# A two-layer GNN and MoE kernel: gate weights transposed one FFN step later, and smaller tiles at the end of layer 1

## What is computed

```python
x = x + gnn0(layernorm(x), edge_weight1)     # weighted mean over in-edges, [h_neigh, x] @ W.T + b
x = x + ffn0(layernorm(x))                   # 8 experts 256 -> 512 -> 256, relu, top 2, softmax
h = relu(layernorm(x) @ Wp.T + bp)           # layer 1: 128 features
agg = sqrt(segment_sum(w * h[src]**2, dst))
x = x + h @ W1.T + b1 + agg @ W2.T + b2
x = x + ffn1(layernorm(x))                   # 8 experts 256 -> 256 -> 256, gelu, residual inside
```

## Time and profile before

| | |
|---|---|
| median of three runs | 2748.9 us |
| the profiled execution | 2746.08 us, span 2744.2 us |
| mean granted TensorE clock | 0.941 |
| busy share: TensorE, VectorE, ScalarE, GpSimd | 83%, 68%, 47%, 62% |
| gather DMAs, GpSimd | 1664, mean 1.01 us |
| chain that ended last, by engine | PE 47%, POOL 24%, DVE 12%, issue 11%, ACT 4% |

### The profile page before, as it was taken

The page is one execution under the profiler, slowest core; times in us unless marked ns, Lnnn a source line. Parts: engine busy times, 40 slices in busy tenths (PEclk is TensorE's granted clock), DMA queues, the critical chain, the costliest instruction groups (busy, mean ns, idle before and its releaser), DMA issues.

```text
span 2744.2 us, 45870 instructions
## 1 busy us (share of the span) xinstructions
PE 2265.4 (83%) x16513; PEld 1420.9 (52%) x16513; DVE 1857.9 (68%) x4929; ACT 1296.2 (47%) x2221; POOL 1710.3 (62%) x1678
## 2 busy tenths in 40 slices
PE   0137999999999999999999734588878778988987
PEld 0124555555555555555558634444444444567876
DVE  8576777778778777787776644355555555667775
ACT  4023455454454554544556601244334444566667
POOL 3677666575575665764430077777777777777760
PEclk9999999999999999999999955699999999999999
DMA  5733333343333333432220032122222222222220
GB/s 208 253 104 110 102 107 103 97 120 88 98 111 92 106 103 97 118 93 82 72 64 21 32 108 62 51 63 70 69 57 63 70 70 63 63 67 71 71 61 11
DMA packets 116317, 237.92 MB, mean 87 GB/s; under 512 B 30434, under 2 KB 70364, under 8 KB 115572
## 3 DMA queue, kind: packets, MB, share of 16 engines
q0 software_dynamic: 66560, 163.68, 21.3%
q1 hardware_dynamic: 49524, 71.26, 7.7%
HBM read 209.16 MB, written 25.67 MB: 86 GB/s over the span
## 4 chain that ended last, share of the span: by engine, by line
PE 47%; POOL 24%; DVE 12%; issue 11%; ACT 4%; DMA 2%; DVEq 0%; POOLq 0%; ACTq 0%; SPq 0%
POOL ring L625 23%; PE psY L757 18%; PE psH L721 17%; PE psM L821 4%; PE psE L703 2%; DVE hsc L1334 1%; PE psE L711 1%; DVE hid L1328 1%; DMA ring<-table,src_s 1%; PE psM L773 1%; PE psE L731 1%; PE psE L705 1%; PE psM L781 1%; ACT L1506 1%; DVE wbuf L1074 1%
## 5 line engine op out<-in xcount | busy, mean ns | idle before, releaser
L625 POOL DMA_INDIRECT ring<-table,src_s x1664 | 1680.7, 1010 | 902.4 <-issue 624.1
L721 PE MATMUL psH<-xnT,wbuf 128*128 128x512 f16 (+2 forms) x4320 | 909.9, 348 | 8.3 <-ACT hid L1517 8.3
L757 PE MATMUL psY<-hsc,wbuf 128*128 128x512 f16 (+2 forms) x4320 | 902.9, 345 | 11.2 <-DVE hsc L1334 6.2
L1517 ACT ACTIVATE hid<-psH,b,scl 128x512 f32<-128x512 f32 (+2 forms) x720 | 503.4, 699 | 761.1 <-PE psH L721 757.8
L1328 DVE TENSOR_TENSOR hid<-hid,cS 128x512 f32<-128x512 f32 (+2 forms) x720 | 427.7, 594 | 452.0 <-ACT cS L1524 310.1
L757 PEld LDWEIGHTS psY<-hsc,wbuf 128*128 128x128 f16 x4320 | 415.5, 99 | 391.4 <-issue 23.6
L721 PEld LDWEIGHTS psH<-xnT,wbuf 128*128 128x128 f16 x4320 | 406.1, 102 | 300.8 <-issue 21.1
L1334 DVE TENSOR_TENSOR hsc<-hid,hsc 128x512 f16<-128x512 f32 (+2 forms) x720 | 423.1, 588 | 0.4 <-ACT hsc L1531 0.3
L711 PE MATMUL psE<-ohbuf,ring 128*128 128x40 f32 x1664 | 251.1, 306 | 186.7 <-DMA ring<-table,src_s 186.5
L1531 ACT ACTIVATE hsc<-hid 128x512 f16<-128x512 f32 (+2 forms) x720 | 392.0, 544 | 27.1 <-DVE hid L1328 26.1
L711 PEld LDWEIGHTS psE<-ohbuf,ring 128*128 128x128 f32 x1664 | 238.3, 219 | 233.4 <-DMA ring<-table,src_s 227.9
(11 more groups left out here) (163 smaller groups left out, 1938.6 us busy)
## 6 DMA issues: line engine op xcount, KB each, us to landing
ring<-table,src_s POOLq DMA_INDIRECT x1664, 2.5
wbuf<-w_in SPq DMA_DIRECT2D x2, 4096.0 KB, 20.7
wbuf<-x_in SPq DMA_DIRECT2D x7, 896.0 KB, 12.7
table<-ring SPq DMA_DIRECT2D x7, 896.0 KB, 3.6
feat<-table SPq DMA_DIRECT2D x11, 512.0 KB, 4.0
xin<-x_in SPq DMA_DIRECT2D x11, 512.0 KB, 3.9
x_d<-x SPq DMA_DIRECT2D x11, 512.0 KB, 3.5
wbuf<-w_in SPq DMA_DIRECT2D x2, 2048.0 KB, 11.2
```

The costliest lines, as they stand in the source:

```text
L625: pool.indirect_dma_start(out=l.ring[:, g % l.R, k, :], out_offset=None, in_=l.table, in_offset=bass.IndirectOffsetOnAxis(ap=src_s[:, c:c ...
L721: last = mm(psH[n % 2][:, 0:l.TT[t]], l.w1(e, i, k, c), x[:, j, k, 0:l.TT[t]], start=(k == 0 and m == 0), stop=(k == KD - 1 and m == 2))
L757: last = mm(psY[d][:, 0:l.TT[t]], l.w2(e, i, c, d), h[:, j, 0:l.TT[t]], start=False, stop=(n == l.M - 1 and m == 2))
L1517: f(hid[(l.M * t + n) % HB][:, 0:l.TT[t]], psH[n % 2][:, 0:l.TT[t]], (ACT.Relu, ACT.Gelu)[l.i], scale=l.un_up, bias=l.b1[:, n // l.HC, n % ...
```

## The change

Two edits. The transposition of the gate weights moves on TensorE from the end of step `at_comb` (29 in layer 0, 13 in layer 1) to the following step, between that step's `up` (which there is the first `up` of the next tile) and its `down`. The wait for `comb_ready` moves from the middle of that step's `down` to the head of `spread_weights` behind it. The place of `weights_copied` on ScalarE and of `gate_weights` on VectorE stays. And layer 1's list of tiles becomes eight of four, six of two, five of one: 19 tiles.

```diff
-ENDS = (([], [2, 2, 1]), ([], [2] * 8 + [1]))
+ENDS = (([], [2, 2, 1]), ([], [2] * 6 + [1] * 5))
@@ def spread_weights(l, t, e):
                 x = NX * t + e
+                if t and e == 0:
+                    pe.wait_ge(l.comb_ready, t + 1)
                 added, copied = l.spread_after[x]
@@ def down(l, t, n, at):
                     for m, (i, j) in enumerate(PARTS):
-                        if d == 0 and m == 1 and at[1] + 2 == l.M and at[0] < l.NT - 1:
-                            pe.wait_ge(l.comb_ready, at[0] + 2)
@@ the loop over steps
                             up(l, t + 1, n + 2 - l.M)
+                        if n == l.at_comb + 1 and not last:
+                            weights_transposed(l, t + 1)
                         if n:
                             down(l, t, n - 1, (t, n))
...
                             logits(l, t + 1)
-                        if n == l.at_comb:
-                            weights_transposed(l, t + 1)
```

## The result

The changed kernel takes 2758.09 us (median of 5 runs, 2754.08 to 2760.52), the kernel before in the same comparison 2745.66 us (2740.91 to 2751.58): ratio 1.0041, 95% interval 1.0023 to 1.0059, 11 us slower. The forecast was 15 us slower. Measured again later, the ratio was 1.0043 (1.0030 to 1.0055).

A forecast was written before the change was run, and what follows sets the result against it. TensorE bounds layer 0, GpSimd's gathers set layer 1's pace up to the last four-block tiles, and the tail is bound by its own instructions. 2746.08 - 13.5 - 4 + 32.4 = 2761.0 us profiled, 2764 us median; range 2746 to 2778.

The forecast's parts named there:

- Edit 1, layer 0: Layer 0's loop: the next tile's first `up` fills TensorE's wait at the transposition; 13.5 us of 16.4 gained.
- rival (c): Layer 0: the wait returns at `spread_weights` because ScalarE's copy comes late; +13.5 us, 2777.5 us; chance 0.05.
- Edit 1, layer 1: Layer 1's tail: waits ahead of the transposition get back at least an `up`; -4 us, bounds 0 and -5.
- Edit 2: Layer 1's end: blocks 44 to 48 become five tiles; tail 202.8 us, 32.4 us more than before.
- wait behind the last gather: Layer 1's end: claimed there is none for the two more tiles to shorten.
- four stretches with their ten sums: Layer 1's end: four one-block stretches of 25.5 us each, plus 6 us for 10 group sums.
- Rival (b): One-block tiles: more latency, TensorE at half clock behind stalls; 28.5 us a stretch, +12, 2776 us; chance 0.12.
- Rival (a): One-block tiles: ScalarE the only bound, sums hidden in TensorE's idle time; tail 182.4 us, median 2743.4 us; chance 0.20.
- lower bound: One-block stretch at layer 1's end: ScalarE's work alone, 21.4 us.
- The sum: Whole kernel: 2746.08 - 13.5 - 4 + 32.4 = 2761.0 us profiled; 2764 us on the median, slower by 15 us.
- second of the two rules: One-block tiles: the Trainium skill's about 81 ns per 128-column matmul gives TensorE 15.6 us; rejected for the trace's 56 ns.

The follow-up runs named there:

- layer-0-only kernel: Transposition moved in layer 0 alone, old list of tiles, against the kernel before: 2732.97 us, ratio 0.9941.
- filled kernel: Changed kernel plus matmuls adding zeros in TensorE's waits of the four one-block tiles that prepare another: 2751.56 us, against 2759.04 us of the changed kernel.
- run without the roots: Changed kernel with copies for the two square roots in preparing layer 1's tiles 15 to 18: 2742.15 us, ratio 0.9975 to the kernel before.

## Why the prediction was right, and which terms were off

**Edit 1, layer 0.** Right in mechanism and nearly in size: 13.5 us forecast, 13.8 in the first trace. The `up` covers 1.28 of 1.29 us, the wait doesn't come back at `spread_weights`, and rival (c) falls: ScalarE waits for the transposition (23.5 us in all), not TensorE for the copy. The layer-0-only kernel had 16.3 us by its median, with an interval of 3.6 us either way; by the stretches its trace has 13.7 us from the second tile on. The first tile's time varied between 112 and 116 us from trace to trace, in kernels of both kinds.

**Edit 1, layer 1.** The term was mis-sized. I took 4 us, with bounds of 0 and 5; the changed kernel's trace was 10.6 us ahead in layer 1 at 2549 us. That trace is the upper end. From layer 0's last transposition to that point the traces without the edit in layer 1 took 1039.0, 1039.5 and 1040.5 us, and the five others with it on these chips 1029.8 to 1035.3 us, so 3.7 to 9.2 us less. The five waits at L843 there, which I had priced, fell from 11.9 us before to 7.3 us in that trace, 4.6 us in all, where the `up`s in front of them are worth 3.9 (1.29 and four times 0.65 us). What I put at nothing is TensorE's own work. In the five stretches from 2355 to 2574 us before, it was busy 199.3 us, in the same ones with the moved transposition alone 191.5 us, with the same instructions: the difference is the granted clock, 0.92 to 0.97 there and 0.96 to 1.00 here. The other traces scatter, 196.1 and 199.6 us without the edit and 191.7 to 196.0 us with it. That the shorter stall keeps the clock up is argued from these columns, and no run isolates it. In the old list the gathers take most of it back; that the new list keeps it I had not seen.

**Edit 2.** The plan held: two-block stretches 37.7 and 35.0 us forecast, 0.65 less each with the moved transposition, 35.6 and 34.7 measured; the end 22.1 and 22.3. The wait behind the last gather was indeed not there: with the gathers out 26 us earlier against the end, or more, the time rose. The term that failed in size is four stretches with their ten sums: 108 us forecast, 114.3 in the first trace and 110.4 in the second. With no sums a stretch took 27.0 and 26.1 us, not 25.5, and the first two took 30.2 and 30.1 us (29.1 and 28.2) with four sums each. What I left out of the likeliest case is the half clock, 0.78 to 0.91 in these stretches. Rival (b) had it with the right place and too high a price, 12 us; the filled kernel shows 5 to 7. Rival (a), ScalarE as the only bound, falls: its work is just the 21.4 us of the lower bound, but it idles for 6 to 9 us more in each stretch. ScalarE's waits from 2620 to 2734 us, the four stretches:

```profile
ACT hsc L1531 <- DVE hid L1328: 10.0, 9, 2.1
ACT hid L1517 <- PE psH L721: 6.0, 9, 2.3
ACT yT L1543 <- PE psY L757: 5.2, 4, 1.4
ACT cT L1510 <- PE psM L843: 5.1, 4, 1.4
ACT cS L1524 <- PE psE L733: 1.4, 4, 0.8
```

They stand ahead of the FFN's own steps, of the output and of the copied gate weights; none stands ahead of a root or an exp. So ScalarE and the other two engines hand the short steps of one block to each other late; how much of that each table load causes is shown only by the run without the roots, above.

**The sum.** +32.4 - 17.5 = +14.9 forecast, +12.1 by the traces, with the gain and the loss both larger than forecast: -24.4 by 2549 us (and two smaller gains in the two stretches behind), and +36.5 after it. By medians +11 to 12 us. List alone +38 us, and the list on top of the moved transposition +31 us, where I had said 32.4. That the sum came within 3 to 4 us is in part luck: the gain was 6.9 us larger in the first trace than the 17.5 us of the forecast, and the loss 4.1 us larger than the 32.4 us, and the two offset each other. Two slips in the working are too small to matter: eleven pieces of 0.65 us that fall to 0.34 us lose 3.4 us, not 3.7, and the 15.6 us that the second of the two rules gives TensorE is below the 21.4 us of ScalarE in a tile that prepares another, not above.

What stays open: how the 31 us divide. Taking the four root loads of a tile away gives back 18 us of the changed kernel, but these loads are also there in tiles that the old list has; at 4.5 us a tile the two that were added account for half of that, 9 us. The clock comes on top (0.86 to 0.90 in the four stretches without the loads, 0.86 to 0.91 with them), so 14 to 16 us of 31 are named. The rest, 15 to 17 us, may be the remaining latency of two more preparations; no run took it apart. And what holds up all engines on the slow chip is open.

## What to carry to other kernels

A wait of a saturated engine for a late small result can be filled by moving the waiting instruction behind the next independent block of the same engine; it gives back the smaller of wait and block, here 1.28 us in each tile of four blocks. The consumer behind it had its own cover here; no run shows the case without. Before a pipeline's last tiles are made smaller, ask whether it is the transfer or the fixed part of each tile that the tail waits for: here, with four table loads for roots, two for exp and a chain of small instructions, a tile took 27 us for one block against 31 for two. Judge an edit beside the others: by the traces, what the moved transposition gains is eaten in part by the gathers with one list and kept with another.

## What the runs showed of the hardware

Adding 384 matmuls made a kernel 7.5 us faster: with TensorE's waits filled, the granted clock stayed at 1.00 in place of 0.86 to 0.89 in the last three of the four stretches. Of the six table loads of a tile those for the roots cost 1.1 us each of their 1.28. Twenty to 36 added matmuls of 128 columns in a row, each with its own weight load, started 56 ns apart at the full clock. GpSimd issued its gathers about 1.25 us apart where nothing held it up. And one chip took 3108 us for the kernel that takes 2749 on others, with 536, 405 and 201 us of waits on ScalarE, VectorE and GpSimd that the profile calls `remote` and that no trace of the others has; the ratios of the two edits were 0.9938 and 1.0085 there and 0.9927 and 1.0139 elsewhere. The list cost less there, and why is open.
